# A ring of 24 result tiles, four neighbouring tokens per partition, and row normalization on ScalarE in the first combine stage

## What is computed

```python
x = x + 0.5 * ffn(layernorm(x), ...)        # f1
x = x + attention(layernorm(x), ...)
x = x + 0.5 * ffn(layernorm(x), ...)        # f2

def ffn(x):                                 # mixture of 8 experts, top 2, and a shared expert
    normed = layernorm(x) * gamma + beta
    probs = softmax(normed @ router_w.T)
    top_v, top_i = top_k(probs, 2); gates = softmax(top_v)
    out = sum over the two experts of gate * (silu(h @ Wg.T) * (h @ Wu.T)) @ Wd.T   # 384 wide
    return out + shared expert (128 wide)
```

## Time and profile before

| | us |
|---|---|
| median of 3 runs | 2221.39 (2219.1 to 2222.46) |
| the profiled execution, its own time | 2220.59 |
| its span in the profile | 2218.8 |
| 0 to 425: f1, route and expert tiles | 425 |
| 425 to 531: f1, combine | 106 |
| 531 to 1738: attention | 1207 |
| 1738 to 2170: f2, route and expert tiles | 432 |
| 2170 to 2219: f2, combine | 49 |

### The profile page before, as it was taken

How to read it: one execution, slowest core, us unless ns; L and a number is a source line. 1 busy time by engine, 2 the same in 40 slices (tenths; PEclk the granted TensorE clock), 3 DMA queues, 4 the chain that set the end, 5 groups by cost and what they waited for, 6 DMA issues and landing times. The chain is left out here.

```text
span 2218.8 us, 64909 instructions
## 1 busy us (share of the span) xinstructions
PE 2034.5 (92%) x22952; PEld 1239.0 (56%) x22953; DVE 1922.7 (87%) x4202; ACT 1265.3 (57%) x2997; POOL 1262.3 (57%) x1873
## 2 busy tenths in 40 slices
PE   7897999777999999999999999999999777989990
PEld 4587999633444444444444444444444565989990
DVE  6984666586999999999999999999999688866666
ACT  3454555345666666666666666666666245545550
POOL 3777765322555555555555555555555367777550
PEclk8998999889999999999999999999999889999995
DMA  5342222277011021101201110121000234422217
GB/s 161 89 133 72 87 80 69 80 228 193 3 40 31 12 40 40 27 15 40 40 19 23 40 40 12 30 59 40 7 2 7 68 94 126 104 80 87 69 50 231
DMA packets 163712, 147.89 MB, mean 67 GB/s; under 512 B 51858, under 2 KB 138002, under 8 KB 162898
## 3 DMA queue, kind: packets, MB, share of 16 engines
q1 hardware_dynamic: 144288, 108.31, 19.6%
q0 software_dynamic: 17280, 35.56, 4.7%
q10 hardware_dynamic: 1874, 0.51, 0.1%
HBM read 87.81 MB, written 60.45 MB: 67 GB/s over the span
## 5 line engine op out<-in xcount | busy, mean ns | idle before, releaser
L1327 PE MATMUL ps_scores<-c_relw,stat_rel 64*64 64x512 f32 x4096 | 938.7, 597 | 0.0
L1394 ACT ACTIVATE probs<-ps_scores,neg_max 128x512 f32<-128x512 f32 x1024 | 695.8, 684 | 397.4 <-DVE neg_max L1369 396.1
L1369 DVE TENSOR_REDUCE neg_max<-ps_scores 128x1 f32<-128x512 f32 x1024 | 645.8, 664 | 10.5 <-PE ps_scores L1327 9.6
L1362 DVE STREAM_TRANSPOSE probs_T<-probs 128x1024 f32<-128x1024 f32 x512 | 627.5, 1226 | 0.0
L1315 PE MATMUL ps_scores<-keys,stat_keys 64*64 64x512 f32 x2560 | 588.2, 595 | 0.5 <-ACT probs L1394 0.5
L1327 PEld LDWEIGHTS ps_scores<-c_relw,stat_rel 64*64 64x64 f32 x4096 | 279.1, 133 | 278.1 <-issue 210.7
L1315 PE MATMUL ps_scores<-c_batch,stat_keys 64*64 64x512 f32 x1536 | 354.1, 597 | 5.0 <-POOL stat_rel L1262 3.0
L1260 POOL TENSOR_TENSOR stat_keys<-queries_by_head,c_mask 128x128 f32<-128x128 f32 x320 | 152.4, 476 | 312.1 <-PE ps_scores L1327 312.1
L1287 PEld LDWEIGHTS ps_values<-probs_T,values_diag 128*32 128x32 f32 x8192 | 208.2, 109 | 205.3 <-issue 204.0
L1287 PE MATMUL ps_values<-probs_T,values_diag 128*32 128x128 f32 x8192 | 276.1, 276 | 1.1 <-DVE probs_T L1362 1.1
L1315 PEld LDWEIGHTS ps_scores<-keys,stat_keys 64*64 64x64 f32 x2560 | 171.5, 132 | 122.7 <-issue 112.6
(11 more groups left out here) (297 smaller groups left out, 3718.6 us busy)
## 6 DMA issues: line engine op xcount, KB each, us to landing
c_batch<-dispatched SPq DMA_DIRECT2D x142, 129.0 KB, 2.2
qkv_record<-f1c_rec SPq DMA_DIRECT2D x16, 768.0 KB, 3.9
f1c_Y<-expert_out SPq DMA_DIRECT2D x32, 256.0 KB, 4.3
f2c_Y<-expert_out SPq DMA_DIRECT2D x32, 256.0 KB, 4.6
c_batch<-qkv_record SPq DMA_DIRECT2D x24, 256.0 KB
keys<-qkv_record SPq DMA_DIRECT2D x20, 256.0 KB
attn_out_T<-attn_out SPq DMA_DIRECT2D x16, 256.0 KB, 2.0
c_Os<-attn_out_T SPq DMA_DIRECT2D x16, 256.0 KB, 3.2
```

Of the source, the lines that this page charges most:

```text
L1327: m = nc.tensor.matmul(out, SR[n // 2 % NS][p, h, :, :].rearrange("p h a -> p (h a)"), R[p, w0:w0 + L], start=False, stop=True)
L1362: nc.vector.transpose(PT[G % 2][:, :, 2 * pair:2 * pair + 2, :, :].rearrange("p r i h a -> p r (i h a)"), Pr[U % NPAIR][:].rearrange("p i ...
L1369: nc.vector.reduce_max(nmx[U % NPAIR][:, n % 2:n % 2 + 1], psS[U % NPAIR][:, n % 2, :], AX, negate=True).then_inc(s_mx, 1)
L1394: nc.scalar.activation(Pr[s][:, n % 2, :], psS[s][:, n % 2, :], ACT.Exp, bias=nmx[s][:, n % 2:n % 2 + 1], accum_out=rs[:, G % 2, tt:tt + 1 ...
```

## The change

Five edits:

1. `YR` becomes 24: slots 2 and 3 of `n0` also serve as result tiles. The waits on earlier scatters move from tile n-16 to tile n-24, the tile with number 16 gets a wait for the dispatch DMAs that read those slots, and the part of DVE's tile program that is written out ahead of the loop grows to 24 tiles, with 24 tiles in the loop body (which is then run once).
2. Step s of the residual stream now holds tokens 512s to 512s+511 with four neighbouring tokens in a partition (token 512s + 4p + j in partition p, group 4s + j). All DMAs between XR or `Y` and DRAM (input, expert results, output) then move runs of 2 KB. The table of token numbers `tid` is permuted to match. Attention still works in natural token order, so the copy to `xT` writes with a step of four floats, and `oproj` reads its stationary operand from `Os` with a step of four floats.
3. In f1's combine the normalization moves from DVE to ACT: x * rs + sh, with rs the reciprocal deviation and sh = -mean * rs. It runs one step earlier in ACT's order, between the copy to `xT` and the three bias additions.
4. POOL computes sh, two more instructions a step.
5. DVE's order in that stage: combine, statistics, aggregate, then transpose V of s-3; and its 19 steps are all written out, with no loop.

```diff
-    XR8, YR, FAR = 8, 16, 4
+    XR8, YR = 8, 24
-        homes = Os + [flat(n0[k][q][:]) for q in range(2) for k in range(TOPK)]
+        homes = Os + [flat(n0[k][q][:]) for q in range(4) for k in range(TOPK)]
...
-                xv = T["x"].rearrange("(n p) d -> p n d", p=P)
-                sp.dma_start(XR[:, 0:8, :], xv[:, 0:8, :]).then_inc(s_xa[0], 16)
+                xv = T["x"].rearrange("(s p j) d -> p s (j d)", p=P, j=JT)
+                xr = XR[:].rearrange("p (s j) d -> p s (j d)", j=JT)
+                sp.dma_start(xr[:, 0:2, :], xv[:, 0:2, :]).then_inc(s_xa[0], 16)
...
-                wait(dve, (s_ld[s.slot(off)], 16 * (s.lap(off) + 1)), (s_st[s.slot(off)], 16 * NS * s.lap(off - 12)))
+                wait(dve, (s_ld[s.slot(off)], 16 * (s.lap(off) + 1)), (s_st[s.slot(off)], 16 * NS * s.lap(off + 4 - YR)))
...
-                    wait(dve, (x_dn, s.n(-1)), (s_st[s.slot(-2)], 16 * NS * s.lap(-14)))
+                    wait(dve, (x_dn, s.n(-1)), (s_st[s.slot(-2)], 16 * NS * s.lap(2 - YR)))
...
+                    if isinstance(s.i, int) and s.n(-2) == 16:
+                        wait(dve, (s_sc[2], 3 * SC), (s_sc[3], 3 * SC))
...
-                    t = nc.tensor.matmul(psE[:, j, :], Os[s % 4][:, j * P:(j + 1) * P], wo[:], start=True, stop=True)
+                    t = nc.tensor.matmul(psE[:, j, :], Os[s % 4][:].rearrange("p (q j) -> p j q", j=JT)[:, j, :], wo[:], start=True, stop=True)
...
-            yv = yd[0:TOPK * TOK, :].rearrange("(k n p) d -> p k n d", k=TOPK, p=P)
+            yv = yd[0:TOPK * TOK, :].rearrange("(k s p j) d -> p k s (j d)", k=TOPK, p=P, j=JT)
...
-                    wait(pool, (s_A, KA * s.n()))
+                    wait(pool, (s_A, KA * s.n()), (s_rs, KN * s.n(-1)))
                     nc.gpsimd.tensor_tensor(ve[:], mv[q][:, :, 1], eps[:], ALU.add).then_inc(s_rs, 1)
-                    wait(pool, (s_rs, 2 * s.n(-1) + 1), (s_C, JT * s.n(-3)))
+                    nc.gpsimd.tensor_scalar(nm[:], mv[q][:, :, 0], -1.0, None, ALU.mult).then_inc(s_rs, 1)
+                    wait(pool, (s_rs, KN * s.n(-1) + 2), (s_C, JT * s.n(-4)))
                     nc.gpsimd.tensor_tensor(rs[q][:], ve[:], mhalf[:], ALU.pow).then_inc(s_rs, 1)
+                    wait(pool, (s_rs, KN * s.n(-1) + 3))
+                    nc.gpsimd.tensor_tensor(sh[q][:], nm[:], rs[q][:], ALU.mult).then_inc(s_rs, 1)
...
-                if s.on(-2, NB):
-                    q = s.slot(-2)
-                    wait(dve, (s_rs, 2 * s.n(-1)), (s_tp, s.n(-3)))
-                    for j in range(JT):
-                        nc.vector.tensor_scalar(xn[s.slot(-2, 2)][:, j, :],
...
-            run_steps(dve, 0, NB + 3, 8, NB, emit)
+            if last:
+                run_steps(dve, 0, NB + 3, 8, NB, emit)
+            else:
+                for n in range(NB + 3):
+                    emit(Step(n // 4, n % 4))
...
-                    nc.scalar.activation(xT[:], psT[:], ACT.Copy).then_inc(s_xT, 1)
+                    nc.scalar.activation(xT[:].rearrange("p (q j) -> p j q", j=JT), psT[:].rearrange("p (j q) -> p j q", j=JT), ACT.Copy).then_inc(s_xT, 1)
+                if s.on(-1, NB):
+                    q = s.slot(-1)
+                    wait(act, (s_rs, KN * s.n()), (s_tp, s.n(-2)))
+                    for j in range(JT):
+                        nc.scalar.activation(xn[s.slot(-1, 2)][:, j, :], flat(XR[:, bass.ds(JT * s.n(-1) + j, 1), :]),
+                                             ACT.Identity, bias=sh[q][:, j:j + 1], scale=rs[q][:, j:j + 1]).then_inc(s_C, 1)
```

More of the change, by code:

```diff
@@ L1031, in combine @@
             ve = sb(c, tag + "_ve", [P, JT])
+            nm = sb(c, tag + "_nm", [P, JT])
+            sh = [sb(c, f"{tag}_sh{q}", [P, JT]) for q in range(4)]
+            KN = 4
             rs = [sb(c, f"{tag}_rs{q}", [P, JT]) for q in range(4)]
@@ L1050, in load @@
                 for k in range(TOPK):
[L1051 removed]
+                    sp.dma_start(Y[q][:, k, :, :].rearrange("p j d -> p (j d)"), yv[:, k, bass.ds(s.n(off), 1), :].rearrange("p o x -> p (o x)")).then_inc(s_ga[q], 16)
             for k in range(2):
@@ L1120, in emit @@
                     wait(dve, (s_A, KA * s.n(-1) + JT))
+                if s.on(-1, NB):
+                    for j in range(JT):
+                        nc.vector.bn_aggr(mv[s.slot(-1)][:, j, :], st[:, j, :]).then_inc(s_A, 1)
                 if s.on(-3, NB):
@@ L1124, in emit @@
                     nc.vector.transpose(rc[q][:, 2 * L:3 * L], Vf[q2][:]).then_inc(s_r, 1)
-                if s.on(-1, NB):
-                    for j in range(JT):
-                        nc.vector.bn_aggr(mv[s.slot(-1)][:, j, :], st[:, j, :]).then_inc(s_A, 1)
-            run_steps(dve, 0, NB + 3, 8, NB, emit)
+            if last:
[3 more added lines that the diff above has]
+                    emit(Step(n // 4, n % 4))
         if last:
@@ L1436 @@
         "ones": np.ones((P, P), _F),
-        "tid": np.arange(TOPK * TOK, dtype=np.uint32).reshape(TOPK, NT, P).transpose(2, 0, 1),
+        "tid": np.arange(TOPK * TOK, dtype=np.uint32).reshape(TOPK, NB, P, JT).transpose(2, 0, 1, 3).reshape(P, TOPK, NT),
         "pads": np.concatenate([np.zeros((SPARE * P, D), np.uint32),
```

15 lines of the change are left out of this document (7 added, 8 removed).

## The result

| | before | changed |
|---|---|---|
| median, us | 2220.33 | 2193.45 |
| ratio (95% interval) | | 0.9882 (0.9868 to 0.9896) |
| span of the profiled execution, us | 2218.8 | 2192.5 |

The changed kernel is 26.9 us faster by these medians. One of its four executions took 3474.23 us at a granted clock of 0.55 and is left out of the ratio; the median of the other three is 2192.51. The forecast was 2186, 34 us less, with a range of 2176 to 2202: the direction and the range hold, the point is 7.5 us off. That is not one error of 7.5 us, as a table by stage shows. Its times are distances between two events that both profiles have, so that the parts add up to the change of the span.

The account below looks back on a forecast made before the run. Bounds: PE in the expert tiles, broken by DVE's waits, and DVE in f1's combine; attention untouched. Gains 17.0 + 7.6 + 2.9 + 6.0 + 1.8 = 35.3 us take 2220.59 to 2185.3, forecast 2186, range 2176 to 2202.

Parts of the forecast that it names:

- The ring: Expert tiles: 24 result tiles remove DVE's wait for a scatter at tile 16, 17.0 us less in f1, 7.6 in f2.
- The loop: f2's expert tiles: DVE's loop body runs once, so two PE gaps at the jump back go, 2.9 us less.
- The steps of four floats: Strided weight loads in `oproj` and strided copy to `xT`: taken as 0 us, with +15 as the other end.
- The prediction's other branch: A weight load taking twice as long and showing fully: about 1 us more per `oproj`, +13 us; copy to `xT` 0 to 2.
- the seven pairs: f2's route: pairs of steps in which DVE waits for `oproj`, priced at 1.4 us each if weight loads slow down.
- the rival of costly steps: Weight loads and the copy to `xT` run at half their rate: 2186 + 15 = 2201 us, chance 0.27.
- f1's combine: Normalization and loop overhead leave DVE: steps of 4.9 us against 5.55, 6 us less in all, bounds 10 and 0.
- The chain of 9.8 us a pair: f1's combine: aggregate(n) over POOL, ACT and DVE to aggregate(n+2) takes at least 9.8 us, 4.9 us a step.
- The 4 us charged for PE's clock: f1's combine: six phases at PE's low clock, 0.7 us charged for each not absorbed, about 4 us against the gain.
- the edges: f1's combine: third combine starts 1.0 us earlier, and last combine to last transpose shrinks from 13.36 to about 12.2, 1.1 less.
- The runs of 2 KB: Loads and stores at four exposed edges: faster DMAs gain about 0.5 us each, 1.8 us together, bounds 0 and 4.
- The rival "slower than before": Strided weight loads in `oproj` cost 0.5 us more each, five times today's: about 2225 us, chance 0.03.

Follow-up runs that it names:

- e5_combine_unrolled: The kernel before with only DVE's program of f1's combine written out instead of looped: ratio 0.9985 to the kernel before.
- e8b_later_transpose: The changed kernel with POOL writing attention output in permuted order, and f1's combine transposing V and storing the record one step later: 2180.11 us, ratio 0.9831.

## Why the prediction was right, and where it was not

**The ring: right.** 17.0 and 7.6 us were read off as a distance of copies; the run with the ring alone shows 16.9 and, with the loop, 10.6. POOL caught up where computed, and nothing was late next. That 17.0 was met to a tenth is luck, since the wait that was removed varied from 13.9 to 16.7 us between kernels.

**The loop: right.** 2.9 us were forecast, and the run that removes only the jump shows 3.4.

**The steps of four floats: wrong.** This is the step that failed: "I take 0 for both, as nearest to the ordinary rows, and keep +15 as the other end". There was no row for it, and the value was chosen by likeness; yet the strided load was the one thing about those rows that was not alike. The prediction's other branch had the mechanism and nearly the size: a load that takes 1.7 times as long, 1.0 us more per `oproj`, +7.4 to 8.6 us in all instead of 13. One of the seven pairs costs DVE nothing (additions at 1811.75 and 1814.96, 3.21 us apart with either load), and where PE ran at the lower clock the plain loads took 333 ns already (before, 1829 to 1831, granted clock 0.50). The copy to `xT` costs 0.48 us and, as put, arrives nowhere in the changed kernel (run with the plain copy). So the rival of costly steps is what happened: its time, 2201, was too high because `oproj` was put at 13 and `xT` at 2 us, where 8 and 0 arrived. The measured 2193.45 lies as far from 2201 as from 2186; that it fell inside the range is in part luck of the other terms, and the rows on the load decide, not the time. The Trainium skill's rule ("Advanced Engine Details and Errata", SBUF Cachelines) was right on both SBUF accesses, at one access per 16 bytes: 192 to 329 ns for the weight load at the higher clock, 597 to 1074 ns for the write. A rule that speaks against the change, with no row against it, deserved more than 0.27.

**f1's combine: the chain right, the sum near by errors that offset each other.** The chain of 9.8 us a pair measured 9.65, so the steps gave 8.6 us and not 7.8. The 4 us charged for PE's clock did not come. In the windows of the stage the granted clock is 1.00 from 440 on, as here, where the kernel before had 0.74 to 0.97 (columns: length, busy PE, PEld, DVE, ACT and POOL, clock, DMA share, GB/s):

```profile
485.00:500.00 15.00, 10.82 (x28) 4.48 (x27) 13.44 (x57) 6.69 (x10) 3.52 (x6) 0.89 0.77 246
```

```profile
455.00:470.00 15.00, 9.84 (x30) 4.66 (x30) 12.65 (x52) 13.34 (x25) 5.69 (x13) 1.00 0.79 279
```

PE is less busy there than before, 9.84 for 10.82 of 15 us, so I can't say from these rows why it kept the clock. In return the edges, where 1.0 and 1.1 us were to be gained, lost 0.5 and 0.1: the distance from the last combine to the last transpose is 13.48 us, not 12.2. And the attribution was wrong: the prediction put the gain on moving the normalization, with the loop as a by-product. By the runs the written-out program alone gives 5.9 of the 8.0 us (4.8 to 6.4 against other kernels with the loop). The move gives 4.8 where the copy to `xT` is strided, but some 2.7 of that only undoes the copy's price, which shows where DVE still normalizes. Part of the 5.9 is a step of 5.95 us ahead of the loop (451.38 to 457.33), of a kind that other looped kernels show too and e5_combine_unrolled does not.

**The runs of 2 KB: about right,** -1.1 us at three of the four edges against -1.5. Kernels with runs of 512 bytes show 13.0 to 13.9 and 12.0 to 12.9 us at the two loads, so the size is not known to better than half a microsecond.

**The rival "slower than before"** is added up wrongly: 128 loads by 0.5 us at two thirds are 43 us, which gives 2229 and not 2225. Nothing hangs on it.

**What was not in the sum:** +2.1 us before the first result copy, +1.3 in attention. Attention's length by profile, without the kernels on the slow chip, is 1206.0 us in three kernels in which the first group of products takes 1.47 us, and 1207.4 to 1208.7 in seven in which it takes 2.02 to 2.79, the kernel before and the changed one among them. Of the edits of the change none lies in that stage. So a part of the spread goes with how fast PE is when it begins: timelines of PE in the changed kernel and in e8b_later_transpose.

```profile
508.92 2.79 PE L1327 MATMUL ps_scores<-c_batch,stat_keys 64*64 64x512 f32 x9 [2.95 <-POOL stat_rel L1274]
```

```profile
504.20 1.47 PE L1328 MATMUL ps_scores<-c_batch,stat_keys 64*64 64x512 f32 x9 [2.95 <-POOL stat_rel L1275]
```

The first result copy stands at 143.3 to 143.8 us in five kernels with the old order of f1's route or its layout alone, and at 141.8 to 145.7 in five with the whole change, whose code for that stage is the same. The two extremes differ in the granted clock of the stretch from 5 to 50 us, 0.81 at 141.8 and 0.77 elsewhere; but not all that spread is explained by it. Whether the change has a part in the 2.1 us stays open; a forecast of this kernel can't be closer than that. With the ring of 16 such a delay is covered: start and f1's tiles together end at 417.0 us in the kernel before and at 414.3 to 415.1 in the three others, since DVE then waits the less for POOL. With 24 tiles it counts in full, and the first two rows of the table together gain 14.8 us, not 16.9.

## What to carry to other kernels

Price edits in the order in which their covers fall: an edit that removes a wait also uncovers all that the wait had hidden, so a cost of "nothing, hidden behind X" must be asked again when another edit of the same change removes X. If an access pattern is new to the trace, no row is nearest to it: give a rule that speaks against it more weight than a likeness until a run says otherwise, and look for a place to permute where it is free, here PSUM's side or a write that already had a step. A wait at the end of a chain of k steps is cut by taking its last link one step later. Here the buffers sufficed, and the price was one more step at the stage's end. And what an edit is worth depends on the others: run the changed kernel without it, and it alone, before a gain is put down to it.
